# Both products of an autoencoder by seven half-size products each, against one pass of eight, in a float32 kernel

## The reference

```python
B, L, D, F = (1024, 2, 1024, 4096)       # the x given has 512 rows
f = jax.nn.relu(jnp.einsum('bld,ldf->bf', x, W_enc) + b_enc)
x_hat = jnp.einsum('bf,lfd->bld', f, W_dec) + b_dec
```

## Time and profile before

| | before |
|---|---|
| time, median of 3 runs | 710.08 us (709.92 to 711.35) |
| the profiled execution: its span | 707.8 us |
| TensorE busy | 701.2 us (99%), 3080 matmuls |
| VectorE busy | 234.5 us (33%) |
| ScalarE busy | 231.3 us (33%) |
| 16 DMA engines, bytes moved | 75.77 MB, mean 107 GB/s |

### The profile page before, as it was taken

The page is one execution under the profiler, slowest core; times in us unless marked ns, Lnnn a source line. Parts: engine busy times, 40 slices in busy tenths (PEclk is TensorE's granted clock), DMA queues, the critical chain, the costliest instruction groups (busy, mean ns, idle before and its releaser), DMA issues.

```text
span 707.8 us, 8006 instructions
## 1 busy us (share of the span) xinstructions
PE 701.2 (99%) x3080; PEld 578.5 (82%) x3080; DVE 234.5 (33%) x260; ACT 231.3 (33%) x308; POOL 0.2 (0%) x4
## 2 busy tenths in 40 slices
PE   8999999999999999999999999999999999999997
PEld 5888888888888888888888888888888888888886
DVE  4333333333333333333333333333333333333330
ACT  5232253222522235223342322232253223322323
POOL 0000000000000000000000000000000000000000
PEclk9999999999999999999999999999999999999999
DMA  8932233223322332332223222322226223221003
GB/s 314 386 103 90 90 106 102 89 89 105 102 89 89 107 100 89 91 112 93 89 90 108 100 90 89 109 99 90 89 96 230 90 91 109 97 89 59 0 1 119
DMA packets 23777, 75.77 MB, mean 107 GB/s; under 512 B 2896, under 2 KB 3408, under 8 KB 23760
## 3 DMA queue, kind: packets, MB, share of 16 engines
q1 hardware_dynamic: 23760, 75.53, 32.4%
HBM read 71.33 MB, written 4.19 MB: 107 GB/s over the span
## 4 chain that ended last, share of the span: by engine, by line
PE 98%; DMA 1%; SPq 0%; ACT 0%; issue 0%; ACTq 0%
PE sums L254 33%; PE sums L256 33%; PE sums L255 33%; DMA w_raw<-w_enc 1%; SPq L113 0%; SPq L107 0%; ACT w_hi L142 0%; ACT out_sb L166 0%; ACT v_hi L141 0%; SPq L95 0%; ACTq L137 0%
## 5 line engine op out<-in xcount | busy, mean ns | idle before, releaser
L254 PE MATMUL sums<-v_hi,w_hi 128*128 128x512 f32 x1016 | 395.3, 389 | 1.7 <-ACT w_hi L142 1.7
L255 PE MATMUL sums<-v_lo,w_hi 128*128 128x512 f32 x1016 | 395.2, 389 | 0.0
L256 PE MATMUL sums<-v_hi,w_lo 128*128 128x512 f32 x1016 | 395.2, 389 | 0.0
L254 PEld LDWEIGHTS sums<-v_hi,w_hi 128*128 128x128 f32 x1016 | 190.8, 188 | 41.6 <-ACT w_hi L142 2.1
L256 PEld LDWEIGHTS sums<-v_hi,w_lo 128*128 128x128 f32 x1016 | 190.8, 188 | 39.6
L255 PEld LDWEIGHTS sums<-v_lo,w_hi 128*128 128x128 f32 x1016 | 190.8, 188 | 39.5
L214 DVE TENSOR_TENSOR w_lo<-w_raw,w_hi 128x1024 fp32r<-128x1024 f32 x127 | 154.7, 1218 | 0.0
L142 ACT CAST w_hi<-w_raw 128x1024 fp32r<-128x1024 f32 x127 | 132.9, 1047 | 0.0
L212 DVE TENSOR_TENSOR v_lo<-f_sb,v_hi 128x512 fp32r<-128x512 f32 x64 | 44.3, 693 | 231.4 <-ACT w_hi L142 231.4
L141 ACT CAST v_hi<-f_sb 128x512 fp32r (+1 forms) x64 | 39.7, 621 | 238.4 <-PE sums L256 238.4
L212 DVE TENSOR_TENSOR v_lo<-x_sb,v_hi 128x512 fp32r<-128x512 f32 x63 | 43.6, 692 | 215.4 <-ACT w_hi L142 215.1
(11 more groups left out here) (10 smaller groups left out, 6.4 us busy)
## 6 DMA issues: line engine op xcount, KB each, us to landing
w_raw<-w_dec SPq DMA_DIRECT2D x64, 512.0 KB, 3.3
w_raw<-w_enc SPq DMA_DIRECT2D x63, 512.0 KB, 4.0
x_sb<-xT SPq DMA_DIRECT2D x16, 256.0 KB, 9.7
outT<-out_sb SPq DMA_DIRECT2D x16, 256.0 KB, 2.1
w_raw<-w_enc SPq DMA_DIRECT2D x4, 128.0 KB, 3.6
b_enc_sb<-b_enc SPq DMA_DIRECT2D x1, 16.0 KB, 3.0
b_dec_sb<-b_dec SPq DMA_DIRECT2D x1, 8.0 KB, 4.6
```

Source lines behind the costliest of these rows:

```text
L254: nc.tensor.matmul(out, w_hi[:, s, cols], v_hi[:, s, :], start=start, stop=False)
L255: nc.tensor.matmul(out, w_hi[:, s, cols], v_lo[:, s, :], start=False, stop=False)
L256: nc.tensor.matmul(out, w_lo[:, s, cols], v_hi[:, s, :], start=False, stop=stop).then_inc(tile_multiplied, 1)
```

## The change

Both products are done by one level of the Strassen scheme: contraction, batch and features are cut in half, and seven products of half-size blocks, of sums and differences of the blocks, take the place of eight. Four products of a chunk use one set of sums ("four" steps), three another ("three" steps). The work is laid out in runs (`RUNS`): `enc1` 4 chunks of four products, `enc2` 4 chunks of three, `dec1` 2 of three, `dec2` 2 of four, `dec3` 2 of four, `dec4` 2 of three. A chunk is 8 steps; each step has 128 rows of both halves of the contraction and 512 output features of both halves. There are 16 chunks and 128 steps, 64 of each kind.

- **Stationary and moving change places.** Stationary are now 128x128 pieces of the activations' forms, moving are 128x512 pieces of the weights. Results come out with batch on the partitions; TensorE transposes them back (`transpose`, 128x128 each, four to a bank), for the encoder's outputs and for the decoder's.
- **Forms**: the sums and differences of activation blocks, by VectorE (`form_sums`), their highs by ScalarE (`form_his`), their lows by VectorE. They are made once per run and pair of blocks (48 times), and stay for all chunks of the run.
- **Weight sums**: a four-product step needs three (T1, T2, T3 in place of three of the four loaded blocks), a three-product step one. From the third step on, the first of these is made by a DMA that POOL issues with an add to its destination (126 of them, 128x512 each); the others by VectorE.
- **Take-out**: the products of a chunk are added into SBUF: copies out of PSUM by ScalarE (26 of 128x1024), sums by VectorE (64 of 128x1024, 36 of them with an operand in PSUM). TensorE's first step of the next chunk waits for them product by product (`FREES`).
- **Loads**: a ring of four steps of 128x2048, each by two DMAs; a step with four products loads all four blocks, one with three loads three of them. The split weights are in a ring of two.
- At the end eight tiles are transposed, biased by ScalarE and VectorE in turn and stored.
- The loops of all engines are written out in full.

```diff
-    SPLIT = 4
-    RAW = 8
+    PAIRS = 8
+    RAW = 4
+    RUNS = [("enc1", True, 4, 0), ("enc2", False, 4, 0), ("dec1", False, 2, 0),
+            ("dec2", True, 2, 0), ("dec3", True, 2, PAIRS), ("dec4", False, 2, PAIRS)]
...
+    FREES = {"enc1": [(True, 1), (True, 2), (True, 3), (False, 1)],
+             "enc2": [(False, 2), (False, 3), (False, 4)],
...
+             "dec3": [(True, 1), (True, 2), (False, 1), (False, 3)]}
+    TILE_STEP = [1, 2, 3, 4, 5, 5, 6, 6]
+    def form_step(r, i):
+        return i - 1 if r == 0 else RUN_LAST[r - 1] + i + 2
...
 SyncE:
+            def load_w(s):
+                if s >= RAW:
+                    sp.wait_ge(lo_done, 2 * (s - RAW + 1))
+                if four:
+                    sp.dma_start(w_pos(s, 0, 2).rearrange("p (h f) -> p h f", h=2),
+                                 w[top:top + P, :, cols]).then_inc(w_loaded[s % RAW], 16)
+                    sp.dma_start(w_pos(s, 2, 2).rearrange("p (h f) -> p h f", h=2),
+                                 w[low:low + P, :, cols]).then_inc(w_loaded[s % RAW], 16)
...
 POOL:
+            for s in range(STEPS):
+                if by_dma(s):
+                    pool.wait_ge(w_loaded[s % RAW], 32 * (s // RAW + 1))
+                    dst, src = (1, 0) if FOUR[s] else (0, 2)
+                    pool.dma_start(w_pos(s, dst), w_pos(s, src),
+                                   accum_op=ALU.add).then_inc(w_summed[s % RAW], 16)
...
 ScalarE:
+            def hi(s, q):
+                act.wait_ge(w_loaded[s % RAW], 32 * (s // RAW + 1))
+                if by_dma(s):
+                    act.wait_ge(w_summed[s % RAW], dma_sums(s))
+                if W_SUMS[s + 1] > W_SUMS[s]:
+                    act.wait_ge(w_sums_done, W_SUMS[s + 1])
+                if s >= 2:
+                    act.wait_ge(multiplied, BLOCKS[s - 2][q])
+                n = 2 if q == 0 or FOUR[s] else 1
+                nc.scalar.copy(split(s, q, 0), w_pos(s, 2 * q, n)).then_inc(hi_done, 1)
...
 VectorE:
+            def w_sums(s):
+                dve.wait_ge(w_loaded[s % RAW], 32 * (s // RAW + 1))
+                if by_dma(s):
+                    if not FOUR[s]:
+                        return
+                    dve.wait_ge(w_summed[s % RAW], dma_sums(s))
...
+                add(w_pos(s, 3), w_pos(s, 3), w_pos(s, 1)).then_inc(w_sums_done, 1)
+                dve.wait_ge(w_sums_done, first + 1)
+                add(w_pos(s, 2), w_pos(s, 2), w_pos(s, 3)).then_inc(w_sums_done, 1)
...
+            for s in range(STEPS):
+                if k == 1 and kind in ("enc2", "dec4"):
+                    for m in range(1, 5):
+                        take_out(n - 1, m)
+                if k == 1 and kind in ("dec2", "dec3"):
+                    take_out(n - 1, 1)
+                for r, i in FORMS_AT.get(s, ()):
+                    form_sums(r, i)
+                if s + 1 < STEPS:
+                    w_sums(s + 1)
+                lo(s, 0)
+                if k == 1 and kind in ("dec2", "dec3"):
+                    take_out(n - 1, 2)
+                    take_out(n - 1, 3)
+                if k == 1 and kind == "enc1":
+                    take_out(n - 1, 1)
+                lo(s, 1)
+                for r, i in FORMS_AT.get(s, ()):
+                    form_lo_direct(r, i)
+                    form_lo_sums(r, i)
...
 TensorE:
-                    nc.tensor.matmul(out, w_hi[:, s, cols], v_hi[:, s, :], start=start, stop=False)
-                    nc.tensor.matmul(out, w_hi[:, s, cols], v_lo[:, s, :], start=False, stop=False)
-                    nc.tensor.matmul(out, w_lo[:, s, cols], v_hi[:, s, :], start=False,
+                for p in range(4 if four else 3):
+                    q = p // 2
+                    if p % 2 == 0:
+                        pe.wait_ge(hi_done, 2 * s + q + 1)
+                        pe.wait_ge(lo_done, 2 * s + q + 1)
+                    if k == 0 and n > 0:
...
+                    for m in range(2):
+                        nc.tensor.matmul(out, v_hi, w_hi, start=k == 0, stop=False)
+                        nc.tensor.matmul(out, v_lo, w_hi, start=False, stop=False)
+                        last = nc.tensor.matmul(out, v_hi, w_lo, start=False, stop=k == PAIRS - 1)
+                    last.then_inc(multiplied, 1)
...
+                for b in range(4):
+                    last = nc.tensor.transpose(sums[:, bank, b * P:(b + 1) * P], src, ident[:])
```

More of the change, by code:

```diff
@@ new lines, in dma_sums, with dve_sums_of @@
+    def dma_sums(s):
+        return 16 * sum(1 for t in range(s % RAW, s + 1, RAW) if by_dma(t))
+    def dve_sums_of(s):
+        own = 0 if by_dma(s) else 1
+        return own + (2 if FOUR[s] else 0)
+    W_SUMS = [0]
+    for s in range(STEPS):
+        W_SUMS.append(W_SUMS[-1] + dve_sums_of(s))
+    TILE_STEP = [1, 2, 3, 4, 5, 5, 6, 6]
+    TILED = [n for n, ch in enumerate(CHUNKS)
+             if n and (CHUNKS[n - 1][1] == "enc2" or CHUNKS[n - 1][1] == "dec4")]
+    def form_step(r, i):
+        return i - 1 if r == 0 else RUN_LAST[r - 1] + i + 2
@@ new lines, in load_x, with store @@
+            def load_x(i, block, loaded):
+                sp.dma_start(whole(block), x_pairs[:, i, :, :]).then_inc(loaded, 16)
+            def store(e):
+                for t in range(8):
+                    if e == 0:
+                        sp.wait_ge(tile_out, 32 + t + 1)
+                    else:
+                        sp.wait_ge(tail_out[t % 2], t // 2 + 1)
+                    row = (t // 4) * D + e * C + (t % 4) * P
+                    src = OUT_PLACE + e * 16 + 2 * t
+                    sp.dma_start(outT[row:row + P, :], place[:, src:src + 2, :]).then_inc(stored, 16)
@@ new lines, in _ @@
+            store(0)
+            store(1)
+            sp.wait_ge(stored, 16 * 16)
+        @block.gpsimd
+        def _(pool):
+            nc.gpsimd.memset(ident[:], 0.0).then_inc(ident_set, 1)
+            pool.wait_ge(ident_set, 1)
+            nc.gpsimd.affine_select(out=ident[:], in_=ident[:], compare_op=ALU.not_equal, fill=1.0,
+                                    base=0, pattern=[[-1, P]], channel_multiplier=1).then_inc(ident_set, 1)
+            for s in range(STEPS):
+                if by_dma(s):
[3 more added lines that the diff above has]
+                                   accum_op=ALU.add).then_inc(w_summed[s % RAW], 16)
@@ new lines, in _ @@
+            for j in range(8):
+                if TILE_STEP[j] + 2 >= PAIRS:
+                    tile(32 + j)
+            for j in range(0, 8, 2):
+                act.wait_ge(transposed, 40 + j + 1)
+                at = OUT_PLACE + 16 + 2 * j
+                col = (j // 4) * (D // P) + 4 + j % 4
+                nc.scalar.activation(place[:, at:at + 2, :], sums[:, TAIL_BANK[j], :], ACT.Identity,
+                                     bias=b_dec_sb[:, col:col + 1]).then_inc(tail_out[0], 1)
@@ L231, in _, with add @@
-            for j in range(1, ENC_K):
-                lo(x_sb[:, j, :], 0, j)
-            with dve.Fori(1, ENC_PASSES) as g:
-                for j in range(ENC_K):
-                    lo(x_sb[:, j, :], g * ENC_ROUNDS, j)
-            for h in range(DEC_PASSES):
-                first = DEC_FIRST + h * DEC_ROUNDS
-                with dve.Fori(0, DEC_ROUNDS) as r:
-                    for j in range(RAW):
-                        lo(f_sb[:, bass.ds(r * RAW + j, 1), :], r + first, j)
+            def add(out, a, b, op=ALU.add):
+                return nc.vector.tensor_tensor(out, a, b, op)
@@ L260, in _, with transpose @@
+            def transpose(n, j, bank):
+                y11, y12, y21, y22 = out_place(n)
+                top, low = (y11, y21) if j < 4 else (y12, y22)
+                for b in range(4):
+                    at = (top if b < 2 else low) + (b % 2) * 2 + (j % 4) // 2
+                    src = place[:, at, (j % 2) * P:(j % 2 + 1) * P]
+                    last = nc.tensor.transpose(sums[:, bank, b * P:(b + 1) * P], src, ident[:])
+                last.then_inc(transposed, 1)
             pe.wait_ge(zeros_set, 1)
@@ L301 @@
+            n = len(CHUNKS) - 1
+            for j in range(8):
+                pe.wait_ge(summed, SUMMED[n] + (3 if j < 4 else 4))
+                if j < 2:
+                    pe.wait_ge(tile_out, 38 + j + 1)
+                transpose(n, j, TAIL_BANK[j])
 def kernel(r_x, L0_rec_W_enc, L0_rec_b_enc, L0_rec_W_dec, L0_rec_b_dec):
```

512 lines of the change are left out of this document (327 added, 185 removed).

## The result

The change takes 717.02 us (median of 4 runs, 712.56 to 719.22) where the kernel before takes 710.2: ratio 1.0081, 95% interval 1.0052 to 1.0111. **Slower by 0.8%**, where 686 us and a gain of 3.4% were forecast. The profiled execution is the fastest of the four (712.56 us, span 710.7), so sums against it are some 4 us short of the median. The other three executions show a lower mean granted clock (0.977, 0.972 and 0.969 against 0.987) and take 2.7 to 6.7 us longer.

A forecast was written before the change was run, and what follows sets the result against it. TensorE bounds the kernel, by instruction count and spacing. 707.8 - 86.9 (matmuls) + 24 (transposes) + 15.6 (head) + 17 (VectorE) + 0 (accumulates) + 6.1 (tail) = 683.6; with 2.3 around the span, 686 us; range 662 to 728.

The forecast's parts named there:

- transposes in the stream: 160 new 128x128 TensorE transposes among the matmuls, taken at 0.15 us each: +24 us.
- head and chunk 0: Start until data lands, VectorE's pace in steps 2 to 7, and clock restarts: +15.6 us over the 7.6 lost before.
- waits in the body: TensorE waiting at chunk boundaries for VectorE's work: +17 us, with accumulating DMAs and ScalarE costed at nothing.
- tail: After the last matmul: one take-out, 32 transposes, then bias, store and end: 9.8 us against 3.7, +6.1.
- the rival with 0.226 to 0.41: Transposes don't overlap: all 192 at 0.226 us give 701 us, at 0.41 give 736; chance 0.16.
- the part on the accumulating DMAs: DMAs take 126 sums off VectorE; an accumulate takes 5 us, under the 7.0 left in four-product steps, so costs 0.
- The ring: Lows of step s-4, load, accumulate, VectorE's sums, lows of step s-1; must close in 16.3 us in four-product steps.
- the accumulate is slow, and the ring sets the pace: Rival: accumulates at 9.7 us make the kernel 750 us, slower than before; decides from about 8.1 us; chance 0.14.
- VectorE in the body: VectorE's take-outs and forms exceed TensorE's time: +4 us each in chunks 11 and 13, +5 in 12, +4 elsewhere: +17.
- The clock: In the head, TensorE idles and matmuls restart slow: two restarts at 1.5 us each, +3.
- The signs that I gave: Right: four-product steps near 5.5 us, accumulates 4 to 6, VectorE busy 480 to 560; wrong: accumulates over 7, waits every step.
- ScalarE at nothing: ScalarE's work, near 355 us of 680, was costed at nothing, covered by 1.5 steps of run-ahead.

The follow-up runs named there:

- e2: The change with VectorE's weight sums of the next step moved behind both lows of the current step, same instructions: 688.36 us, ratio 0.9693 to the kernel before.
- e4: The change with the accumulating DMA made a plain copy, so the first weight sum is left out: 687.45 us (one run).
- e9: The change, VectorE's order kept, with each load waiting only for the low it needs and four-product accumulates only for the first load: 689.44 us, ratio 0.9718.
- e11: e10 plus the split waits of e9, halves cut for 4 KB rows, accumulates from step 6, take-outs ahead of the forms' sums: 677.7 us, ratio 0.955.
- e1: The change without accumulating DMAs, all weight sums made by VectorE: 709.99 us, ratio 0.9994 to the kernel before.
- e12: e11 with VectorE's two weight sums in chunks 10 to 13 over 128 columns instead of 512, the rest left out: 667.44 us, ratio 0.9403.
- e10: e2 with ScalarE's first high of a four-product step no longer waiting for VectorE's two weight sums: 683.01 us, ratio 0.9597.
- e6: The change without accumulating DMAs and with VectorE's weight sums behind the lows, as in e2: 728.48 us, ratio 1.0236.

## Why the prediction was wrong

In the terms of the sum, against the profiled span of 710.7 us (a chunk's loss is its length less 43.4 or 32.6):

| term | forecast | measured |
|---|---|---|
| 2688 matmuls at 0.2262 | 608 | 608 (undisturbed steps last 5.44 and 4.08: 609) |
| transposes in the stream | 24 | about 20 (chunks 5 to 8 and 15, 3.9 to 4.3 each) |
| head and chunk 0 | 23.2 | 17.6 + 8.6 = 26.2 |
| waits in the body | 17 | 46.6 |
| tail | 9.8 | 9.4 |

Matmuls, head and tail are right within 3 us. (The head's sum has a slip: its own 6.04 less 0.3 against 5.43 makes 1.9 us over six steps, not 2.5.) **Transposes**: 32 at the end take 3.71 us, the last of them 0.27, so they are spaced 0.11 us:

```profile
702.13 3.71 PE L538 MATMUL sums<-ident,place 128*128 128x128 f32 x32 [0.91 <-DVE place L339]
```

In the stream four of them lengthen a step by 0.49 us (4.57 against 4.08). My 0.15 was dear, and the rival with 0.226 to 0.41 is out. The 275 ns of the Trainium skill (TensorE: Matmul & The Clock Gate, Part 4) agrees with the 272 ns that one lasts here; but that is a duration, and what a stream pays is the spacing.

**The step that failed** is in the part on the accumulating DMAs: "Under 7.0 it costs **0**; the cover is the four-deep ring." The ring was the right object, and "the accumulate is slow, and the ring sets the pace" was a rival. What was wrong is the ring's budget. Here are the means of the 24 steps of chunks 1 to 3, from the starts and landings in the trace, as the lines from 70.61 to 88.87 show them for one step:

| part of the ring | forecast | measured |
|---|---|---|
| load, first issue to both landed | 5.5 | 7.2 |
| landing to POOL's issue | 0 | 0.3 |
| accumulate, issue to landing | 5 | 6.5 |
| sums of VectorE | 1.4 | 1.4 |
| two lows | 2.4 | 2.4 |
| together, for 16.3 available | 14.3 | 17.8 |

So the ring doesn't have 2.0 us to spare; it is 1.5 us too long. By the rival's own formula, 1.5 / 3 for each of 24 steps, that is 12 us, and chunks 1 to 3 lost 14.9. In 18 of the 24 steps VectorE begins the sums within 0.2 us of the landing, so nearly the whole wait is the ring; in e2 it does so in none, and the accumulates land 2.5 us before they are needed. Of the 14.9 us, e2, e4 and e9 leave 1.4, 2.1 and 0.8. The waits in the body that lie neither here nor in chunks 11 to 13 (9.7 of the 46.6 us, in chunks 4, 9, 10 and 14) were not taken apart; e11 leaves 4.4 of them.

Two terms are too small, the load by 1.7 us and the accumulate by 1.5. The load's rate, 402 GB/s, is from a stretch of before in which POOL issued no DMA; without accumulates (e1) the same two loads take 6.2 us in these chunks, so about half of the 1.7 comes from the second stream. The forecast also said that loads and accumulates fill about 60% of the DMA time; its own numbers (1.57 MB against 402 GB/s x 5.43 us) make 72%, and the shares measured in these chunks are 0.82 to 0.85. The rival put its point of decision at an accumulate of 8.1 us, since it took the load's 5.5 as given: with the load at 7.2 and 0.3 to the issue, some 5.0 are left for the accumulate, not 7.0.

**VectorE in the body.** Forecast +13 for chunks 11 to 13, measured 22.0. In e11, with the ring out of the way, 11.3 us are left (47.3, 47.1 and 47.1), near the +13, and e12 takes 10.1 of them away with the work. So VectorE's part was sized about right. Of the other half e2 takes most by the order alone (14.0 us are left there) and the further edits of e11 the rest; how much of it is the clock's isn't shown.

**The clock.** I gave it 3 us in the head and nothing in the body. The 17 us at half rate in the body cost up to 8.5, and they are part of the 46.6 above. That is a price of waits, and the rows of before, with no wait in the body, have none of it.

The signs that I gave hardly told the failure. The accumulates landed in 5.9 us by the median, inside the 4 to 6 given as right, and in 6.5 in chunks 1 to 3, not over the 7 given as wrong; VectorE waited for them 36 times, not in every step, and was busy for 522 us, as forecast. What spoke against the forecast were the mean of a four-product step in chunks 1 to 3, 6.05 us for 5.5, and TensorE's first matmuls on data at 17.6 us for 13 to 15. ScalarE at nothing was not quite right either: TensorE waited for it 8.9 us in ten places. (What e10 gained, 5 us over e2, came from a wait of ScalarE on VectorE.)

## What to carry to other kernels

Where a DMA takes over a sum from an engine, look at what stands behind the wait for it, and put that wait last among what the engine could do. Add up the ring that the buffer closes (free, load, add, use, free), and take the landings as they are under the load that the new kernel makes: here the same ring was 14.3 us by the rates of a quieter time and 17.8 in fact, for 16.3 available. When a large forecast gain doesn't come, reorder before undoing: here the same instructions in another order were worth 4%. Without the DMAs that order was worse (e6), so the two have to be tried together.
